# Turning the even batches earlier in the queues of VectorE and ScalarE, and four copies of eight on each

## The reference

```python
x = x + einsum('bct,bcd->bdt', x, w0[idx])        # one 128x128 matrix per batch, chosen by an index
q, k, v = x @ Wq.T, x @ Wk.T, x @ Wv.T            # 16 heads of 64, 128 positions
attn = softmax(mask(beta * q @ k.T / 8))
x = x + (attn @ v) @ Wo.T
```

## Time and profile before

| | |
|---|---|
| median of 3 runs | 1558.62 us (1558.28 to 1558.96) |
| the profiled execution | 1558.96 us, its span 1557.5 us |
| mean granted clock of TensorE | 0.998 of full |
| busy share PE / PEld / DVE / ACT / POOL | 99% / 84% / 66% / 54% / 56% |
| PE waits in the pair stage | one, of 0.5 us |
| turning (L1254) | 26 instructions |
| copies TT to XR | 130 on DVE (L1260, mean 287 ns, median 284), 78 on ACT (L1069) |

### The profile page before, as it was taken

One profiled execution on the slowest core, in us unless ns is written; L12 is line 12 of the kernel. 1 busy time (PEld: TensorE's weight loads), 2 busy tenths in 40 slices (PEclk: granted clock), 3 DMA queues, 4 the chain that ended last, 5 costly groups with the idle time before them and its releaser, 6 DMA issues.

```text
span 1557.5 us, 23477 instructions
## 1 busy us (share of the span) xinstructions
PE 1547.1 (99%) x7459; PEld 1302.0 (84%) x7459; DVE 1034.9 (66%) x1891; ACT 840.9 (54%) x2286; POOL 866.6 (56%) x752
## 2 busy tenths in 40 slices
PE   9999999999999999999999999999999989999999
PEld 7888888888888888888888888888888878888887
DVE  5867677664477777777767777777777644555553
ACT  6666566652466666666655666666666622222220
POOL 1555665662365566557655576575577545555552
PEclk9999999999999999999999999999999999999999
DMA  9968988866766677767677466677665696444442
GB/s 324 335 230 278 319 307 296 294 254 231 273 190 198 201 214 209 205 184 191 182 240 229 147 179 202 194 200 200 180 188 157 237 366 226 162 168 163 162 167 83
DMA packets 192300, 341.46 MB, mean 219 GB/s; under 512 B 23986, under 2 KB 116402, under 8 KB 185010
## 3 DMA queue, kind: packets, MB, share of 16 engines
q1 hardware_dynamic: 191026, 331.59, 66.2%
q10 hardware_dynamic: 1152, 8.39, 1.4%
HBM read 184.70 MB, written 134.22 MB: 205 GB/s over the span
## 4 chain that ended last, share of the span: by engine, by line
PE 95%; DVE 2%; DMA 1%; SPq 1%; POOL 0%; issue 0%; ACT 0%; DVEq 0%; POOLq 0%
PE p_PJ L768 22%; PE p_PJ L769 22%; PE p_PJ L770 22%; PE p_SC L770 6%; PE p_SC L769 6%; PE p_SC L768 6%; PE p_PV L873 4%; PE p_LP L768 1%; PE p_PV L768 1%; PE p_PV L770 1%; PE p_PV L769 1%; PE p_LP L770 1%; PE p_LP L769 1%; DVE t_WSL L1285 1%; DVE t_TS L1281 1%; DMA out<-t_xr 0%
## 5 line engine op out<-in xcount | busy, mean ns | idle before, releaser
L769 PE MATMUL p_PJ<-t_XL,t_WH 128*128 128x512 f32 x1008 | 394.2, 391 | 0.0
L768 PE MATMUL p_PJ<-t_XH,t_WH 128*128 128x512 f32 x1008 | 394.2, 391 | 0.0
L770 PE MATMUL p_PJ<-t_XH,t_WL 128*128 128x512 f32 x1008 | 392.1, 389 | 0.0
L1118 ACT ACTIVATE t_PP<-t_PP,t_st 128x128 f32<-128x128 f32 x512 | 199.5, 391 | 174.9 <-DVE t_st L1314 173.3
L1438 POOL TENSOR_TENSOR t_PP<-t_PP,t_st 128x512 f32<-128x512 f32 x128 | 133.2, 1041 | 205.8 <-DVE t_st L1318 205.8
L770 PEld LDWEIGHTS p_PJ<-t_XH,t_WL 128*128 128x128 f32 x1008 | 189.3, 188 | 40.5
L768 PEld LDWEIGHTS p_PJ<-t_XH,t_WH 128*128 128x128 f32 x1008 | 190.0, 188 | 33.8
L769 PEld LDWEIGHTS p_PJ<-t_XL,t_WH 128*128 128x128 f32 x1008 | 190.0, 188 | 32.3
L1332 DVE TENSOR_REDUCE t_AT<-p_PV 64x256 f32<-64x512 f32 x252 | 171.3, 680 | 24.5 <-ACT t_AC L1136 12.1
L1444 POOL TENSOR_TENSOR t_AT<-t_AT,t_AC 128x256 f32<-128x256 f32 x126 | 117.1, 929 | 126.2 <-DVE t_AT L1332 126.2
L1441 POOL TENSOR_TENSOR t_PS<-t_PT,t_PS 128x512 fp32r<-128x512 f32 x122 | 157.6, 1292 | 0.0
(11 more groups left out here) (259 smaller groups left out, 3597.7 us busy)
## 6 DMA issues: line engine op xcount, KB each, us to landing
t_XH<-xth_scratch SPq DMA_DIRECT2D x56, 512.0 KB, 6.4
t_XL<-xtl_scratch SPq DMA_DIRECT2D x56, 512.0 KB, 6.7
t_PT<-t_TB SPq DMA_DIRECT2D x580, 32.0 KB, 2.3
v_scratch<-t_VR SPq DMA_DIRECT2D x64, 256.0 KB, 4.6
xth_scratch<-t_XH SPq DMA_DIRECT2D x16, 1024.0 KB, 4.5
xtl_scratch<-t_XL SPq DMA_DIRECT2D x16, 1024.0 KB, 6.8
t_VX<-v_scratch SPq DMA_DIRECT2D x32, 512.0 KB, 5.6
at_scratch<-t_AT SPq DMA_DIRECT2D x126, 128.0 KB, 3.4
```

The lines of the kernel that those rows point to most:

```text
L768: pe.matmul(bank, lh, rh, start=first, stop=False, skip_group_check=goes_on)
L769: pe.matmul(bank, lh, rl, start=False, stop=False, skip_group_check=goes_on)
L770: return pe.matmul(bank, ll, rh, start=False, stop=last, skip_group_check=goes_on)
L1118: act.activation(PP[:, u, h, :], PP[:, u, h, :], ACT.Exp, bias=st[:, 0, u, h:h + 1], scale=1.0, accum_out=st[:, 1, u, h:h + 1]).then_inc(a ...
```

## The change

The turning, the copies, and the high and low parts of the even batches move to earlier places in the queues of DVE and ACT. `p` here is the step of the batch's first product, which is -2 in the terms above: turning goes from 8.5 and 12 to 2.25 and 5.5, the copies from 9.5 and 13 to 3.5 and 6.5, the high parts from 15.5 and 16.25 to 8 and 8.75, the low parts from 16.5 and 17.25 to 9 and 9.75. Besides, ACT takes four of the eight copies of a half and DVE four.

```diff
                 if turned_by_dve(bb):
-                    l0_turn.put(p + (10.5, 14)[h], (bb, h))
-                    l0_move.put(p + (11.5, 15)[h], (bb, h))
-                    x_high.put(p + 17.5 + 0.75 * h, (bb, h))
-                    x_low.put(p + 18.5 + 0.75 * h, (bb, h))
+                    l0_turn.put(p + (4.25, 7.5)[h], (bb, h))
+                    l0_move.put(p + (5.5, 8.5)[h], (bb, h))
+                    x_high.put(p + 10 + 0.75 * h, (bb, h))
+                    x_low.put(p + 11 + 0.75 * h, (bb, h))
...
-        ACT_MOVES = ((0, 5, 7), (0, 5, 7))
+        ACT_MOVES = ((0, 2, 5, 7), (0, 2, 5, 7))
```

## The result

The changed kernel takes 1581.64 us (median of 4 runs, 1580.28 to 1583.79) against 1558.45 us before: 1.0149 times as long, 95% interval 1.0133 to 1.0165. That is 23.2 us more, where 19.7 were forecast. The profiled execution took 1581.07 us, its span 1579.6 us, its mean granted clock 0.998.

What follows compares the result with a forecast made beforehand. PE, busy 99% of the span, was taken as the bound; 3.01 (pair 2) + 8 x 1.49 + 4 x 1.19 = 19.7 us on the profiled 1558.96 gave 1578.7, median 0.34 lower: 1578.3 us, range 1567 to 1586.

Steps and rivals of the forecast that it cites:

- The 1.8 us of slack: In pair 8, the first gather on DVE ended 1.8 us before product 3 started on PE in the old order.
- the step that rested on two rows: DVE's half 0 copies alternate with POOL's instructions: 3.3 us for four copies that take 1.22 alone; chance 0.58.
- The rival of copies in one go: DVE's half 0 copies run together once the lock is theirs: loss 11.3 us, time 1569.9 us; chance 0.16.
- that of copies that don't wait: DVE's copies don't wait for POOL, so only pair 2 pays, 1.2 us: 1559.5 us; chance 0.11.
- the loss per pair: PE's wait at product 3 for the late gather: 1.49 us in pairs 5 to 12, 1.19 in 3, 4, 13, 14.
- upper bound (5 us more): Turning's wait for DVE's last copy 0.1 us more, POOL's blocks at plain durations: 0.1 + 0.3 to 0.4 a pair.
- It just passes: In pair 8, ACT's L1061 ends at 213.14 behind the half 0 copies; product 2 wants it at 213.29.
- What costs nothing: 26 copies going from DVE to ACT, and high and low parts following the late gather with 2.5 us to spare.
- the likeliest case: Alternation of copies and POOL as worked out, with no fall of the clock: 1575 to 1583.5 us; chance 0.58.
- the rival (0.12 for both its forms): PE's granted clock falls behind new waits in the pair stage: once 1582 us (0.07), in most pairs 1624 us (0.05).
- a fall in pair 2: PE's clock falls once, in pair 2, where gaps of 1.2 and 1.8 us are close: 1582 us; chance 0.07.
- a fall in all pairs: PE's clock falls in all 13 pairs: 45 us more, 1624 us; chance 0.05, given for most pairs.

Runs made afterwards that it cites:

- after_fill: The changed kernel with five extra 128x512 matmuls on PE before the wait of product 3 in pairs 3 to 14; 1581.31 us, ratio 1.0151.
- half1_back: The changed kernel with half 1's turning, copies, high and low parts back at their old places, half 0 still early; 1561.07 us, ratio 1.0021.
- copies_behind: The changed kernel with half 1's four copies moved behind the first gather and high and low parts at their old places; 1562.49 us, ratio 1.003.
- short_pool: The changed kernel with POOL's two subtractions for odd batches from 7 on cut from 512 to 32 columns; 1561.93 us, ratio 1.0023.
- parts_back: The changed kernel with the high and low parts back at their old places, turning and copies still early; 1582.34 us, ratio 1.0159.
- moves_only: The kernel before with only the copies shared four on ACT and four on DVE, all places as before; 1558.23 us, ratio 0.9999.
- places_only: The kernel before with all the new places, but still three copies on ACT and five on DVE; 1598.37 us, ratio 1.0254.

## Why the prediction was right

**What bounds, and which slack is used up.** Before, PE has no idle time in pairs 3 to 14; after, it has it at exactly the first matmul of product 3, and after_fill shows that it is idle time. The 1.8 us of slack read from the earlier trace rows decide: with the gather 0.7 us ahead of product 3 (half1_back) or right at the edge (copies_behind) most of the loss is gone. One reading was off and bears on nothing: of PE's other waits, one (0.8 us) is at 25 us and not before 10.

**Copies against POOL.** This was the step that rested on two rows. For pair 8 the prediction had the copies of half 0 end 1.04, 1.52, 2.82 and 3.30 us after they start; measured are 1.03, 1.50, 2.79 and 3.26. With short_pool they end after 1.51. The rival of copies in one go (it had the first four end 1.97 us after they start) and that of copies that don't wait are both out. By the Trainium skill ("SBUF — State Buffer", section "Who interferes with whom") whoever issues first has the shared ports for the whole instruction. The trace agrees, with the interleaved ends above.

**The size of the loss.** The forecast was 19.7 us, measured are 23.2. The mechanism held; the term that was too small is the loss per pair: 1.49 us forecast, 1.75 measured in pairs 5 to 12 (24.47 us from turning to turning, 196.25 to 220.72, less 22.72). Of the 0.26, the trace shows three pieces. Turning half 1 starts 0.13 after DVE's own last copy (224.73 to 224.86), where 0.03 was counted, and 0.05 more comes in the rest of the chain: the gather ends at 228.17, 0.15 later in the pair than forecast. PE restarts worse: its second matmul of product 3 is at 228.62, undisturbed it would be at 226.92; 1.70 late with the gather late by 1.48, so 0.22 on top where the one wait of the kernel before had given 0.16. And the matmuls after a wait start 0.23 apart for a while, not 0.2275, which I take for the last 0.05. In pairs 3, 4 and 13 it is 1.43 (in pair 3, 99.05 to 123.20), where 1.19 was forecast. Pair 2 lost 3.17 (product 0 of pair 3 is at 96.18 and not at 93.57, though PE came out of its first wait 0.56 earlier, at 73.55 and not 74.11) where 3.01 was forecast. 3.17 + 8 x 1.75 + 4 x 1.43 = 22.9 us, against 23.2 between the medians. It is a little too much for these two executions, since pair 14's wait is listed at 0.92 us and not at 1.06: the first instruction of ACT on L1113, behind the pair stage, starts at 412.34 and not at 390.21, 22.1 later, which with the 0.56 makes 22.7. The prediction's upper bound (5 us more) had room for it, though only in part for the reasons it gave: it had named 0.1 a pair for the wait of turning for DVE's own last copy, which came, and POOL's longer durations, which didn't; the slower restart of PE it hadn't named.

**Product 2.** "It just passes" was right to 0.1 us: it starts at 223.97, in its place, but the next matmul follows after 0.31, not 0.23. This and the wait of 1.1 us in pair 2 make most of the 2.6 us of half1_back; 1.2 of them go when L1061 is put ahead, and what remains is the wait for L1269 that takes its place in pair 2. In the changed kernel only pair 2 pays for L1061, since in the others product 3 waits for the gather anyway.

**What costs nothing.** The earlier high and low parts (parts_back) and the fourth copy on ACT (moves_only) cost nothing that shows. In the new places, the fourth copy on ACT saves 0.62 us a pair, and as places_only shows, it also keeps the gaps short enough for the clock.

**The clock.** It didn't fall in the pair stage of the changed kernel's profile (1.00 from 73.5 to 390 us), so the likeliest case held. But the rival (0.12 for both its forms) was near: with gaps listed 0.7 to 0.8 us longer it fell behind five of twelve.

## What to carry to other kernels

When everything is hidden behind one engine, moving work earlier in another engine's queue can gain no more than that engine still waits, 0.5 us here, and can lose much more. Read the slack of each wait of the bounding engine, in microseconds and not in steps, and sum what the move puts ahead of the releasing instruction. Price that chain with what the other engines do at the new time: four copies that took 1.2 us in a quiet place took 3.3 beside GpSimd, since one GpSimd instruction passed between any two of them. Where such work must be early, place it behind the instruction that the bounding engine waits for, or where GpSimd has only short instructions or none.

## What the runs showed of the hardware

- VectorE's copies and GpSimd's instructions took strict turns, one each, as long as both had work (pairs 2 and 8 of the changed kernel). A 32x256 copy, which takes 0.28 us alone, ended 0.14 to 0.15 us after GpSimd's instruction; GpSimd's 128x128 one lasted 0.50 to 0.51 in place of 0.46 with a copy ahead of it, and its 128x512 one 1.33 in place of 1.29. The short copies bore nearly all of the waiting: 2.0 us for four of them, against 0.13 us for GpSimd's three.
- The block transposition on VectorE (0.71 us) ran beside GpSimd's 128x512 subtraction with both at their plain durations (220.72 and 221.06 above).
- PE's granted clock fell behind idle gaps of only 1.8 to 2.1 us as listed, one gap in 25 us: behind five of twelve in places_only, and behind none with the gaps filled by seven matmuls. Gaps of the same 2.1 us had no fall behind them in four pairs, and neither had the one of 2.6 us in pair 2; what decides between them stays open. With gaps listed at 0.9 to 1.3 us it stayed at 1.00 in the changed kernel. The prediction had priced a fall in pair 2 and a fall in all pairs, but not one in some of them.
